# Cross attention core: value products of two key tiles in one block, and the turn, reciprocal and turn back of the head sums two steps later

## The reference

```
scale = 1.0 / np.sqrt(HEAD_DIM).astype(np.float32)
logits = jnp.einsum('bqhd,bkhd->bhqk', q, k) * scale
w = jax.nn.softmax(logits, axis=-1)
attn = jnp.einsum('bhqk,bkhd->bqhd', w, v)
attn = attn.reshape(b, n, N_HEADS * HEAD_DIM)
return attn @ Wout + bout
```

## Time and profile before

| | |
|---|---|
| Median of 3 runs | 2104.45 us (2103.2 to 2104.84) |
| The profiled execution | 2111.76 us, span of its instructions 2110.0 us |
| Busy in the span | PE 1963.1 us (93%), DVE 1353.1 (64%), ACT 1022.5 (48%), POOL 706.1 (33%) |
| ACT exponentials of the cross core (L1355) | 512, mean 598 ns |
| DVE maxima of the cross core (L1404) | 248 records, mean 1212 ns |
| PE value products of the cross core (L1245) | 1024 records, 137.2 us covered |

### The profile page before, as it was taken

How to read it: one execution, slowest core, us unless ns; L and a number is a source line. 1 busy time by engine, 2 the same in 40 slices (tenths; PEclk the granted TensorE clock), 3 DMA queues, 4 the chain that set the end, 5 groups by cost and what they waited for, 6 DMA issues and landing times. The chain is left out here.

```text
span 2110.0 us, 32325 instructions
## 1 busy us (share of the span) xinstructions
PE 1963.1 (93%) x10831; PEld 1381.2 (65%) x10831; DVE 1353.1 (64%) x2805; ACT 1022.5 (48%) x1730; POOL 706.1 (33%) x610
## 2 busy tenths in 40 slices
PE   7998999978799999998999799988999999999998
PEld 5876676756433434334777566667787888877876
DVE  6454666557799797986878566645232234677775
ACT  3423544345378685765543444435322221477775
POOL 0002756436513232323566466531000000133433
PEclk9997999989899999999999799999999999999999
DMA  6647776257665555443474876636020216443342
GB/s 205 216 151 172 165 174 155 94 182 261 249 165 118 140 119 138 120 104 102 188 250 179 198 168 154 144 110 245 20 100 1 80 46 260 150 73 70 66 78 36
DMA packets 151993, 297.73 MB, mean 141 GB/s; under 512 B 24722, under 2 KB 43284, under 8 KB 150740
## 3 DMA queue, kind: packets, MB, share of 16 engines
q1 hardware_dynamic: 114052, 242.29, 38.8%
q10 hardware_dynamic: 29040, 34.74, 6.4%
q0 software_dynamic: 8736, 18.62, 4.8%
HBM read 181.55 MB, written 102.50 MB: 135 GB/s over the span
## 5 line engine op out<-in xcount | busy, mean ns | idle before, releaser
L1355 ACT ACTIVATE cross_c_prob<-bank 128x512 f32<-128x512 f32 x512 | 271.0, 598 | 114.6 <-PE bank L1204 113.4
L1404 DVE TENSOR_REDUCE row_max<-bank 128x2 f32<-128x1024 f32 x248 | 290.8, 1212 | 24.8 <-PE bank L1166 23.8
L1874 PE MATMUL bank<-moe_hT,moe_w 128*128 128x512 f32 x1056 | 250.3, 393 | 7.5 <-DVE moe_w L2163 7.5
L1204 PE MATMUL bank<-stack 56*128 56x512 f32 (+4 forms) x768 | 224.0, 433 | 15.0 <-DMA stack<-first_c_max_rows 5.5
L1874 PEld LDWEIGHTS bank<-moe_hT,moe_w 128*128 128x128 f32 x1056 | 199.1, 189 | 50.1 <-issue 7.8
L1166 PE MATMUL bank<-stack 48*128 48x512 f32 (+4 forms) x720 | 184.7, 442 | 26.9 <-PEq L71 13.5
L1204 PEld LDWEIGHTS bank<-stack 56*128 56x128 f32 (+1 forms) x768 | 114.3, 195 | 143.7 <-ACT cross_c_prob L1355 69.1
L1352 ACT ACTIVATE rotary_c_prob<-bank 128x512 f32<-128x512 f32 (+1 forms) x176 | 94.1, 559 | 122.4 <-PE bank L1207 122.1
L1352 ACT ACTIVATE first_c_prob<-bank 128x512 f32<-128x512 f32 (+1 forms) x176 | 94.0, 558 | 120.9 <-PE bank L1207 118.2
L1166 PEld LDWEIGHTS bank<-stack 48*128 48x128 f32 (+1 forms) x720 | 92.7, 197 | 90.9 <-DVE row_max L1404 46.1
L1400 DVE CUSTOM_DVE_ANT_0 first_c_masked<-bank,later 128x128 f32<-128x128 f32 (+3 forms) x240 | 107.1, 484 | 63.3 <-PE bank L1166 62.9
(11 more groups left out here) (402 smaller groups left out, 4453.3 us busy)
## 6 DMA issues: line engine op xcount, KB each, us to landing
qk_parts<-first_p_parts SPq DMA_DIRECT2D x32, 512.0 KB, 2.6
stack<-qk_parts SPq DMA_DIRECT2D x64, 256.0 KB, 7.1
qk_parts<-cross_p_parts SPq DMA_DIRECT2D x32, 512.0 KB, 2.7
stack<-qk_parts SPq DMA_DIRECT2D x256, 64.0 KB, 2.6
qk_parts<-rotary_p_parts SPq DMA_DIRECT2D x32, 512.0 KB, 2.7
moe_gate_up_e<-in_experts_gate_up SPq DMA_DIRECT2D x8, 1408.0 KB, 10.3
moe_raw<-in_shared_packed SPq DMA_DIRECT2D x11, 768.0 KB, 8.8
stack<-qk_parts SPq DMA_DIRECT2D x16, 512.0 KB, 6.2
```

The costliest lines, as they stand in the source:

```text
L1204: last = nc.tensor.matmul(tiles[:, h], k_stack[slot][r : r + ALL_ROWS, at, m * P : (m + 1) * P], q_stack[slot][r : r + ALL_ROWS, at, q0:S] ...
L1355: nc.scalar.activation(probability(g, m, j), psum[bank_at["score", n]][:, 0:S], ACT.Exp).then_inc(s.exp_done, 1)
L1404: nc.vector.tensor_reduce(row_max[:, g % 2, m, j - 1 : j + 1], c.banks[:, first : first + WIDE, :], AX_X, ALU.max).then_inc(s.max_done, 1)
L1874: last = nc.tensor.matmul(psum[bank][:], weights(pa, f, k), hT[p % 2][:, pb, k, :], start=m == 0, stop=m == len(steps) - 1)
```

## The change

In the cross core alone, the value products of key tiles 0 and 1 are issued together behind step 11, and those of tiles 2 and 3 together behind step 3 of the next group. Before, each tile had a place of its own: tile 0 behind step 7, 1 behind 11, 2 behind 15 and 3 behind 3 of the next group. DVE's turn, reciprocal and turn back of the group before move from steps 4, 6 and 8 to 6, 8 and 10, and the probability slots go from 8 to 14. The number of instructions of each kind stays. The other two cores have their table in the same line as before.

```
-PROB_SLOTS = 8
+PROB_SLOTS = 14
...
-        FLIP_STEP, NORM_STEP, BACK_STEP = (4, 6, 8) if cross else (5, 6, 7)
+        FLIP_STEP, NORM_STEP, BACK_STEP = (6, 8, 10) if cross else (5, 6, 7)
...
-        VALUES_AT = {13: (0, (0, 1)), 4: (1, (2, 3))}
+        VALUES_AT = {11: (0, (0, 1)), 3: (1, (2, 3))} if cross else {13: (0, (0, 1)), 4: (1, (2, 3))}
...
         def values_behind(g, step):
 
-            if causal:
-                back, tiles = VALUES_AT.get(step, (0, ()))
-                return [(g - back, m) for m in tiles if g >= back]
-            n, beat = divmod(g * N16 + step - VALUES_LAG, HEADS_AT_ONCE)
-            return [divmod(n, TT)] if beat == 0 and 0 <= n < GROUPS * TT else []
+            back, tiles = VALUES_AT.get(step, (0, ()))
+            return [(g - back, m) for m in tiles if g >= back]
```

## The result

The change made the kernel slower: 2169.93 us median (2158.06 to 2174.66, 4 runs) against 2104.07 us (2103.2 to 2104.84, 4 runs), a ratio of 1.0293 with a 95% interval of 1.0271 to 1.0315. The direction was forecast, the size was not: 66 us between the medians (62 by the ratio) in place of 22, outside the range.

A forecast was written before the change was run, and what follows sets the result against it. Two nearly equal chains, PE with ACT (10.92 us a plain group) and DVE's queue (10.64), were taken as the bound; 17.6 + 3.6 + 0.8 gave 22 us on the median, 2126 us, 8-in-10 range 2112 to 2136.

The forecast's parts named there:

- The loop of PE and ACT: Cross core, scoresT and exponentials between value blocks: 5.44 us against 5.22, twice a group, +0.4 us a group.
- DVE behind the two blocks: Cross core, DVE idle before maxima: 1.0 us behind the step 3 block, 0.2 behind the step 11 block.
- the sum for a plain group: Cross-core group without projection: 10.64 + 1.0 + 0.2 + 0.2 = 12.0 us, so +1.1 us.
- Groups with projection: Cross core: gain of 1.05 us at the residual add, losses behind it and behind step 3; +0.3 a group.
- the walk's: Stepping the order forward with trace durations: projection groups 14.1 us old, 14.4 new; plain groups 11.0 and 12.0.
- Probability slots: Cross core: they end no wait; 14 slots needed, cost and gain 0.
- SP's queue: Cross core: stack loads end near 13.6 us, maxima ready to send at 13.7; free just in time, cost 0.
- What bounds the kernel now: Cross core, plain groups: two nearly equal chains, PE with ACT 10.92 us, DVE's queue 10.64; PE clock 1.00.
- The sum of the mechanisms: Whole kernel: 17.6 us plain groups, 3.6 with projection, 0.8 last two, first two 0; together 22 us.
- the dearer case: Rival: both DVE idle times at upper bound, +0.8 at projections; 35 us more, 2139 us; 12 in 100.
- Switches of PE: Cross core: each value block less saves PE 0.3 us, twice a group, 64 in all; counts only inside the chains.
- the rival that PE decides: Rival: 64 fewer blocks at 0.3 us make it faster, 2085 us; with its half way form (2100) 5 in 100.

The follow-up runs named there:

- The run with two products more: Changed kernel with the score products of heads 10 and 11 made twice in the cross core, 2 more a group: 2155.79 us, ratio 1.0227.
- the mixed kernel: Kernel before, with tiles 0 and 1 merged behind step 11 only in the 12 groups with projection, 14 slots: 2100.45 us, ratio 0.9979.
- the one with eight products more: Changed kernel with the score products of heads 8 to 15 made twice in the cross core, 8 more a group: 2154.52 us, ratio 1.0256.

## Why the prediction was wrong, step by step

- **The loop of PE and ACT, DVE behind the two blocks, the sum for a plain group**: right where the clock stayed up. 12.1 us against 12.0; idle 1.13 and 0.23 against 1.0 and 0.2. The run with two products more has groups of 12.07 as well.
- **Groups with projection**: right in size where the clock stayed up. 14.8 against 14.45 is +0.35, where I had +0.3, and the gain at the add and the loss behind it were both there. The terms that I listed give only 0 to 0.2; the 0.3 was the walk's.
- **Probability slots**: right, shown by the run with the slots alone.
- **SP's queue**: right within 0.2 us, and it cost nothing.
- **What bounds the kernel now** is the step that failed. I read a PE clock of 1.00 and took it for a constant of the stretch, when it changed with the order. All steps after it price PE's passes at the upper clock, the second tile at 0.87 us and a block of two at 1.9; behind a fall the block took 3.04. The sum of the mechanisms, 22 us, has a term for the clock that was put at nothing without a reason and measured some 45 us: 92 us at the lower clock, in 26 falls of mostly 1.6 us each. From transposes to transposes, plain groups grew by 38 us in all where I had 17.6, those with projection by 16 where I had 3.6, and the first three by 10, for the first two of which I had 0. I named no rival with it; the dearer case was made of waits and ended at 2139. The direction was right for the reason given, but that reason accounts for only 21 of the 66 us.
- The trace of before had a warning that I didn't read. Its first core, which has long had merged blocks, loses the clock now and then. The view by stretches there:

```profile
354.00:356.10 2.10, 1.73 (x9) 1.53 (x10) 1.14 (x5) 1.12 (x2) 2.10 (x2) 1.00 1.08 242
356.10:359.50 3.40, 3.40 (x26) 2.26 (x29) 1.81 (x6) 1.68 (x3) 0.14 (x1) 0.50 1.07 208
359.50:363.00 3.50, 3.42 (x27) 2.38 (x19) 2.73 (x10) 1.87 (x5) 1.18 (x3) 1.00 1.01 218
```

  Right ahead of 356.1 PE had waited 1.3 us for a DMA. That a stretch with gaps is followed by one at 0.50 could be read there.
- **Switches of PE**: as a forecast for the whole, the rival that PE decides had the wrong sign. That a value block less saves PE 0.3 us was not measured by itself; the mixed kernel's gain of 0.2 us in groups with projection fits with it, and fits with the shorter wait at the residual add too.

The page on the clock in the Trainium skill, TensorE: Matmul & The Clock Gate, Part 1, says that the gate is set by how busy PE has been of late. The runs agree: adding products to the changed kernel took falls away (26 to 16, 13 and 6) and taking products out of the kernel before brought them (none to 7 stretches).

What stays open is what decides how many falls an execution has. The changed kernel's runs differ by 16 us, the one with eight products more by 19. Only one execution of each kernel has a trace, but every run has its mean granted clock, and the changed kernel's four runs stand in its order: 0.950 at 2158.06 us, 0.947 at 2167.89, 0.942 at 2171.96 and 0.941 at 2174.66. A mean lower by 0.009 is 39 us more at half the clock, and half of that, 19 us, is near the 16 (an estimate from these runs). So the spread is mostly time at the lower clock. Products were added only in the stretch from step 12 to 3; that the same number elsewhere in the group would not help was not tried. Nor was a version found in which the fully merged order keeps the clock throughout, so its 21 us at full clock are shown by groups and by the sum above, not by a whole run.

## What to carry to other kernels

When a change gathers PE's dense work into fewer, longer blocks, ask what is left between them: a stretch in which PE only follows other engines can cost it the upper clock, and then the dense block that comes next pays (here 3.04 us in place of 1.92). The granted clock of before is no constant to carry into a forecast; look in the same trace for stretches as thin as the new ones, in any phase, and read what the clock did there. And a value product between two waits is not only a delay: in the order of before it filled PE while ACT and DVE worked, and the clock stayed up.

## What was not expected of the hardware

- The clock fell with PE covered by products for 3.20 of 3.60 us (659.3 to 662.9). PE need not be idle for it, and the covered share of a stretch does not tell that its clock is safe: the first 0.4 us of these were still the value block before, the rest 12 short products spread over 3.2 us.
- Doing more was faster and doing less was slower: 4 needless products a group took 11 to 13 us off the changed kernel (2157 against 2170), and half of the value products left out put 0.5% on the kernel before.
- In the changed kernel the falls come once a group with great regularity, groups of 13.65, 13.67, 13.67, 13.66, 13.66 us, while a run of two groups kept the clock and took 11.8 and 12.1, with PE's order and waits the same to 0.01 us up to where the others fell. I did not find what lets such groups through.
